# A new hand-out order for five engines: the same pieces, planned for four cases of TensorE's clock instead of three

## What is computed

```python
# L0 and L3: linear attention (16 or 8 heads)
q = softmax((xn @ Wq + bq).reshape(...), axis=-1)
k = softmax(masked(xn @ Wk + bk).reshape(...), axis=time)
y = einsum(q, einsum(k, v));  x = x + silu(film(layernorm(y))) @ W_out + b
# L1: softmax attention, 16 heads of 16, 256 x 256 scores
att = softmax(q @ k.T + mask, axis=2);  y = att @ v;  x = x + silu(film(layernorm(y))) @ out_w + b
# L2: two state space scans, forward and backward in time, E = 512 channels, N = 16 states
delta = softplus(dlt @ Wdt.T + bdt);  dA = exp(delta * A);  dBu = delta * B * u
h = dA * h + dBu;  y = sum_n(h * C)         # over 256 steps
out = (silu(mx) * (z1 + z2)) @ Wf.T + bf + skip;  x = x + gate * out
```

## Time and profile before

| | us |
|---|---|
| median of three runs | 4681.6 |
| the profiled execution | 4666.2 |
| its span, first to last instruction | 4664.4 |
| VectorE busy in it | 4085.4 |
| GpSimd busy | 3926.7 |
| TensorE busy | 3850.9 |
| ScalarE busy | 3671.9 |
| to the first scan | 436.7 |
| from there to the first scan of the last but one batch | 3937.0 |
| from there to the end | 290.7 |

### The profile page before, as it was taken

How to read it: one execution, slowest core, us unless ns; L and a number is a source line. 1 busy time by engine, 2 the same in 40 slices (tenths; PEclk the granted TensorE clock), 3 DMA queues, 4 the chain that set the end, 5 groups by cost and what they waited for, 6 DMA issues and landing times.

```text
span 4664.4 us, 73193 instructions
## 1 busy us (share of the span) xinstructions
PE 3850.9 (83%) x26068; PEld 2522.2 (54%) x26068; DVE 4085.4 (88%) x5552; ACT 3671.9 (79%) x8678; POOL 3926.7 (84%) x1836
## 2 busy tenths in 40 slices
PE   4867888888888889888888888888888888888665
PEld 3644555555555555555555555555555555555333
DVE  4313899999999999999999999999999999999985
ACT  0135788888898888888889888888888888888763
POOL 0003899999999999999999999999999999999995
PEclk7777899999999999999999999999999999999876
DMA  4002444444454444445454434445454444444441
GB/s 121 3 7 69 102 100 102 113 110 113 104 119 114 105 98 102 113 110 121 103 115 111 107 93 106 113 110 118 103 119 111 104 97 104 113 113 115 111 106 35
DMA packets 338585, 470.58 MB, mean 101 GB/s; under 512 B 56474, under 2 KB 166150, under 8 KB 338218
## 3 DMA queue, kind: packets, MB, share of 16 engines
q1 hardware_dynamic: 338218, 465.91, 42.9%
HBM read 378.71 MB, written 86.56 MB: 100 GB/s over the span
## 4 chain that ended last, share of the span: by engine, by line
PE 37%; ACT 25%; DVE 20%; POOL 8%; issue 7%; DMA 1%; SPq 0%; DVEq 0%; POOLq 0%; ACTq 0%
PE ps L170 14%; ACT ps L699 7%; DVE ps L714 6%; POOL S_X L758 5%; PE ps L375 5%; PE ps L394 4%; PE ps L793 4%; DVE S_X L714 4%; PE ps L160 3%; DVE A_sm L428 3%; POOL S_X L771 2%; DVE S_X L729 2%; PE ps L403 2%; PE ps L538 2%; ACT T_q L153 1%
## 5 line engine op out<-in xcount | busy, mean ns | idle before, releaser
L758 POOL TENSOR_TENSOR S_X<-S_slot,S_bc 128x1024 f32<-128x1024 f32 x1024 | 2392.0, 2361 | 33.3 <-PE ps L793 28.6
L699 ACT ACTIVATE ps<-S_slot,acol 128x256 f32<-128x256 f32 x4096 | 1736.2, 466 | 184.7 <-DVE S_X L729 127.2
L714 DVE TENSOR_TENSOR_SCAN ps<-ps,S_X 128x512 f32<-128x512 f32 x1088 | 1297.2, 1212 | 64.4 <-ACT ps L699 44.7
L714 DVE TENSOR_TENSOR_SCAN S_X<-ps,S_X 128x512 f32<-128x512 f32 x960 | 1148.7, 1208 | 31.3 <-ACT ps L699 24.8
L771 POOL TENSOR_TENSOR S_X<-S_X,S_bc 128x1024 f32<-128x1024 f32 x480 | 1132.7, 2363 | 49.7 <-DVE S_X L714 49.6
L729 DVE TENSOR_TENSOR S_X<-ps,S_bc 128x512 f32<-128x512 f32 x1088 | 724.0, 676 | 8.9
L793 PE MATMUL ps<-S_X,sum 128*32 128x256 f32 x8192 | 631.8, 412 | 38.8 <-POOL S_X L771 29.1
L394 PE MATMUL ps<-A_qP,A_kP 32*128 32x256 f32 x2048 | 338.2, 454 | 103.4 <-DMA A_qP<-A_ring 62.3
L428 DVE TENSOR_REDUCE A_sm<-ps 128x4 f32<-128x1024 f32 x256 | 312.7, 1222 | 95.9 <-PE ps L375 89.7
L793 PEld LDWEIGHTS ps<-S_X,sum 128*32 128x32 f32 x8192 | 203.0, 114 | 321.1 <-issue 186.4
L375 PE MATMUL ps<-A_kP,A_qP 32*128 32x256 f32 x2048 | 298.2, 409 | 52.4 <-DVE A_sm L428 32.4
(11 more groups left out here) (293 smaller groups left out, 7181.3 us busy)
## 6 DMA issues: line engine op xcount, KB each, us to landing
S_slot<-scr_dd SPq DMA_DIRECT2D x1024, 256.0 KB, 4.5
scr_dd<-C_dd SPq DMA_DIRECT2D x64, 1024.0 KB, 6.8
S_bc<-scr_bc SPq DMA_DIRECT2D x256, 256.0 KB, 6.6
L_xin<-in_x SPq DMA_DIRECT2D x32, 256.0 KB
C_mod<-scr_mod SPq DMA_DIRECT2D x32, 256.0 KB, 6.1
scr_x<-A_x SPq DMA_DIRECT2D x32, 256.0 KB, 5.8
T_x<-scr_x SPq DMA_DIRECT2D x32, 256.0 KB
out_x<-xs SPq DMA_DIRECT2D x32, 256.0 KB, 6.8
```

Source lines behind the costliest of these rows:

```text
L699: ins = a.activation(B["bank"][half_at(b, u, i)][:, n * T:(n + 1) * T], B["slot"][:, s, j, 0, :], ACT.Exp, scale=K.k["acol"][:, s, LINES * ...
L714: v.tensor_tensor_scan(line(x if u in ON_POOL else decay), line(decay), line(x), 0.0, ALU.mult, ALU.add).then_inc(S.scan.sem, 1)
L758: g.tensor_tensor(B["X"][:, u % RING], B["slot"][:, s, :, 1, :], rep(B["bc"][:, s, q, :], 1, LINES), ALU.mult).then_inc(S.b.sem, 1)
```

## The change

The diff touches only the strings. `FIRST` has new orders on every engine, from letter 110 on for TensorE, 142 for VectorE, 38 for ScalarE, 14 for GpSimd and 5 for the sync queue. The sync queue's `FIRST` is shorter by 11 letters, and its `TURN` begins at another place, so that the two join with no piece lost. Each `TURN` holds the same number of each letter as before. The number of instructions, their waits and their buffers are the same.

```diff
--- before.py
+++ after.py
@@ -1480,30 +1480,30 @@
 
 FIRST = {
     "PE": (
-        "WWWWWWWWWWWWWWWLLLLWLWWWWWLWWLWWWWWWWWWWWWWLWWWWWWLWWWWWWWWWWWWWLAAAAAAAAAAAAAAAAAAAAAAAAAALALLLALLLLLLAAAAAACACAACACACA"
-        "ACAAAAACAAAACAACAACCLALLCLALLLLLCLSASAAAAACACSASSACASCACAACASSASASASACASSASASASCASSACAACSSSSSCLASLSLCLSSALLSSLSSSSLLCSSS"
-        "LSTASAAAAACACSASSATCASC"),
+        "WWWWWWWWWWWWWWWLLLLWLWWWWWLWWLWWWWWWWWWWWWWLWWWWWWLWWWWWWWWWWWWWLAAAAAAAAAAAAAAAAAAAAAAAAAALALLLALLLLLLAAAAAAACACACACACA"
+        "ACAAAAACAAAACAACAACCLALLCLALLLLLCLSASAAAAASACSASCACSACACAACASSASASSASSACASASAACASSSACASASCSSCSSSLALSLSCLALSLSSLSSLSLCSSS"
+        "LSTASAAAAASACSASCACSATC"),
     "DVE": (
         "WWWWLWWWWWWWWWWWWWWWLWLWWWWLWLWWWWWWWWWWWWWWWWWLWWWWWWWWWWWWWWLWLWWWWWWWWWWWWWWWWWWWWWWWLWAWWWAAAAAAAAAAALLLLLLLLALACCAA"
-        "AAAAAACAAALLLLLLCLLASSPPLSASSPCSSPSCSPSSPASASASPAPSASASPASASSPGSCPSPSSSSPPSSSSPSPSSPSSPSSSPSPSSSPAGASPASLSPSSPSLLSSPLPSS"
-        "SLSGPPSSSSPSPLC"),
+        "AAAAAACAAALLLLLLCLLASPSLPASSSCPSPSSCSPSSPASASASPASPASASPASASSPGSCPSPSSSPSPSSSSPPSSSPSPSSSSPPSSGSSAPAPSASLSPSSPSLLSSPLSPS"
+        "SSLPSPGSSSPSLPC"),
     "ACT": (
-        "LLLWLLLLLLLLLLAAAAAAAAAAAAAAAAAAALLAALALALLLLLLLLLAACAAACAACCCCCCCACCAAAAACAACAAACCALLAACCLALALLLLCCCLLLLSLSCCCSCSSSASAC"
-        "SAASSACSAACSSCSSCSCSSCSCCSACCSSSASSASSASSASSACSASSSASCASSSASSSACSCSSASLSLSASSACSCLSALSASLSLSSLSLCSCSSSSC"),
-    "Pool": "LALCCCACSLSSSPCCCSSPSSSPSSSPSSPCSPSSSPPSSSSSSPPPSSSPSSAPSSPC",
-    "SP": "LAWWLAACCLACCCssCAsCsSCSLACSCCSStSssCAsCsSCSLACSCCSS",
+        "LLLWLLLLLLLLLLAAAAAAAAAAAAAAAAAAALLAAALALLLLLLLLLLAACAAACAACCCCCCCACCAAAACAAACAAACCALLACAALALLLLLCCCCLLLLLSSCSCSCCSASACA"
+        "SSSASASCAASCSSCCSSCCSSSSCCACSCSSASSASSASSASSCASASSSASCASSSASSSACSSCSSALSLSACSASALSASLSSSLLSSLSLSCCCCSSSS"),
+    "Pool": "LALCCCACSLSSSCPCCSSPSSPSSSSPSSPCSPSSSSPPSSSSSPPPSSSPSSAPSPSC",
+    "SP": "LAWWALACCCACLssCCACssCSSCASCLSStSssCCACss",
 }
 
 TURN = {
-    "PE": "ACATACASSATSASASTACASTSATSATSATSCATSSACAACSSSTSSCLASLSLCLSSALLSSLSSSSLLCSSSLSTASAAAAACACSASSATCASC",
+    "PE": "ACATACASSATSASSASSTACTASASTATATCASSSATCASASCSTSCSSSLALSLSCLALSLSSLSSLSLCSSSLSTASAAAAASACSASCACSATC",
     "DVE": (
-        "SLLSPSSPSPPASSGPPLSASSPCSTTSPSCTSPSSPASASASPAPSASASTPASTASSPTGSCPSPSTSSSPPSSSSPSPSTSPTTSSPSSSPSPSSSPAGASPASTLSPSSPSLLSSP"
-        "LPSSSLSGPPSSSSPSPLC"),
+        "LSLSAPSSPSPPSGPSLPASSSCPSTTTPSSCSPSSPASASASPASPASASTPATSASSPTGSCPSPSSSPSPTSSSSPPSSTSPTTSPSSSSPPSSGSSAPAPSASTLSPSSPSLLSSP"
+        "LSPSSSLPSPGSSSPSLPC"),
     "ACT": (
-        "LSLLLSLSCCCSCSSSASACSAASSACSAACSSTCSSTCSCSSCSCCTSACCSSSTASSASTSASSATSSACTSASSSASCTASSTSTASSSATCSTCSSASLSLSASSACSCLSALSAS"
-        "LSLSSLSLCSCSSSSC"),
-    "Pool": "SPSLSSSPCCCSSPSSSPSSSPSSPCSPSSSPPSSSSSSPTPPSSSPSSAPSSPC",
-    "SP": "tSssCTAsCsSCSLACSCCSS",
+        "LSLLLLSSCSCSCCSASACASSSASASCAASCSSCTCSSTCCSSSSCCTACSCSSASTSASSTASSASSTCATSASSSASCTASSSTASTSSATTCSSCSSALSLSACSASALSASLSSS"
+        "LLSSLSLSCCCCSSSS"),
+    "Pool": "SPSLSSSCPCCSSPSSPSSSSPSSPCSPSSSSPPSSSSSPTPPSSSPSSAPSPSC",
+    "SP": "CSSCASCLSStSssCTCACss",
 }
 
 ONCE = (w_pe, w_dve, w_act, w_sp)
```

## The result

The changed kernel takes 4566.1 us, the median of four runs (4562.65 to 4569.19), against 4681.0 us for the kernel before (4666.38 to 4683.03). The ratio is 0.9762, with a 95% interval of 0.9745 to 0.9778: 114.8 us, 2.4% less. The forecast was 4640 us with a range of 4598 to 4686.

The account below looks back on a forecast made before the run. VectorE was taken as leading, 95.1% busy in steady turns, waiting on chains through TensorE and ScalarE. Terms summed to 1.71 us per turn, taken as 1.2, times 28 turns 34 us: 4632, plus 8 offset, 4640; range 4598 to 4686.

Parts of the forecast that it names:

- A10's term: VectorE's reciprocal (L433) after the turned attention output: its wait goes, 0.80 us per turn, bounds 0 to 0.80.
- The maxima: VectorE's score maxima A2 to A7: the first one's wait goes, 0.26 us per turn, bounds 0 to 0.5.
- the sum cut from 1.71 to 1.2: All terms, us per turn: cut because VectorE, arriving earlier, would meet late exponentials at S41 to S43.
- T8 charged with +0.45: VectorE's masked state (L259): wait grows by about 0.45 us per turn, with S15 and S14 ahead on TensorE.
- S37: VectorE's scan, where ScalarE waits for TensorE's C8, moved ahead: its 0.76 us wait falls by 0.57 per turn.
- the clock term: Half-clock matmuls at TensorE's T5 in long turns: net 0 per long turn, bounds -1.0 to +2.2 us.
- GpSimd and the sync queue at 0: Moves in these two queues: counted 0, the sync queue with bounds -0.3 to 0.3 us per turn.
- T11's 0.39: VectorE's last add of a layer (L279): its wait goes, 0.39 us per turn, bounds 0 to 0.39.
- G4 and L9: For these, TensorE's S36 and L10 come about 0.35 us late, charged against the gain at scan S9.
- The waits only change places: Rival: new tight places on ScalarE return the gains; 0 to 0.3 us per turn, 4672 us, chance 0.23.
- The long turns go too: Rival: filled TensorE idle and S27 ahead of T5 keep the clock up or hide it; 4605 us, chance 0.16.
- The new turn falls into step with the clock: Rival: the half-clock stretch meets T5 in every turn, making the kernel slower; 4730 us, chance 0.11.

Follow-up runs that it names:

- the middle stretch: Kernel before with TensorE's stretch S10 to S16 and ScalarE's S27 to T7 in the changed kernel's order: 4633.9 us, ratio 0.9829, mean turn 129.80 us.
- Filling the wait: Kernel before with two float32 matmuls that nobody reads added ahead of A16's wait on TensorE: 4636.4 us, ratio 0.9921.
- The experiment: Changed kernel with GpSimd's and the sync queue's strings of the kernel before: 4590.9 us, ratio 0.9812.

## Why the prediction was wrong in size

**Right: the bound, and where the largest waits go.** VectorE's work of 124.7 us per turn stayed but for 0.4 us, and the waits in its turn were what there was to win. A10's term was 0.80, measured 0.79. In a plain turn of the changed kernel (timeline, columns as in rows 5):

```profile
1802.33 1.13 PE L394 MATMUL ps<-A_qP,A_kP 32*128 32x256 f32 x8 [1.78 <-ACT A_ring L471]
1803.39 1.11 PE L160 MATMUL ps<-ident,T_q 128*128 128x128 f32 x4
1804.29 3.16 PE L170 MATMUL ps<-C_xT,wcz 128*128 128x256 f32 x8
1807.38 1.93 PE L403 MATMUL ps<-A_ring,A_vA 128*32 128x256 f32 x32
1809.38 0.60 ACT L476 ACTIVATE A_kP<-ps 128x512 f32<-128x512 f32 x1
1811.44 0.35 DVE L433 RECIPROCAL A_srec<-ps 128x32 f32<-128x32 f32 x1
```

Beside the earlier trace rows: T10's row (L160) has no bracket where 2.02 us of waiting stood, the reciprocal has none where 1.17 stood. TensorE now waits 1.78 for exponential A16 in front of A24, because it arrives early. A24 takes 1.13 us in place of 2.08 and C9 3.16 in place of 3.78. In plain turns A24 starts 73.9 us after the turn's first scan, and 76.4 to 78.0 before, more than twice the 1.1 us that I had given it: the idle time in front of it is not the only one that was filled. The clock has a part in A10's gain as well: in most plain turns before, TensorE ran at the lower level from about 76 us on, behind T10's wait, and in the changed kernel this stretch is half as long. The maxima (0.26 predicted, 0.29 measured) and TensorE's wait before L9's product, which I said would stay, agree too; in the same turn of the changed kernel it is 5.0 us:

```profile
PE ps L160 <- ACT T_q L153: 5.0, 1, 5.0
```

**Wrong: the sum cut from 1.71 to 1.2.** I argued that VectorE, arriving earlier, meets exponentials with 0.35 to 0.5 us of margin. The waits of the terms I listed fell by 2.58 us per turn, more than the uncut sum. The margins were those of the old order. ScalarE's string had been moved with the others, and its own waits fell by 3.86 us per turn in total, which I didn't work out. The scans S41 to S43, which I had feared for, don't wait in the changed kernel. The cut cost 0.51 x 28 = 14 us of the error.

**Wrong: T8 charged with +0.45.** I counted the pieces that come in front of T8 on TensorE and not the waits that they fill. By the matched pieces TensorE waited 0.30 us before A17 and 0.60 before A19; both are 0 in the changed kernel. In plain turns T8 starts 64.4 us after the turn's first scan in place of 65.3 to 67.0, with more work in front. The wait on VectorE fell by 0.24, and T9's went (0.14). S37 gave 0.76, not 0.57. Together the two steps are mis-sized by 1.02 us per turn, the largest single part. Which piece brings T8 forward is open. The filled waits are not enough: with the middle stretch on two engines TensorE waits 0 before A17 and A19 as well, and T8's wait stays at 0.37; T6 alone took 0.08 off it. S12 and S13 ahead of T5 are needed, since T5 ahead of them brings the wait back from 0.13 to 0.43, but the middle stretch has them there too. S37's gain, in turn, needs only the middle stretch on two engines, which brought 0.62 of it.

**Wrong: the clock term at 0.** S27, S28 and S30 lost 0.59 us of waits per turn. The long turn of the changed kernel:

```profile
1647.75 1.13 PE L394 MATMUL ps<-A_qP,A_kP 32*128 32x256 f32 x8 [1.62 <-DMA A_qP<-A_ring]
...
1654.76 2.05 PE L170 MATMUL ps<-L3wv,T_xT 128*128 128x256 f32 x4
...
1657.93 0.84 ACT L302 ACTIVATE T_v<-ps,T_pc 128x256 f32<-128x256 f32 x2 [2.34 <-PE ps L170]
1660.83 1.22 DVE L714 TENSOR_TENSOR_SCAN S_X<-ps,S_X 128x512 f32<-128x512 f32 x1 [1.87 <-ACT ps L699]
```

The wait for the DMA and T5 at 2.05 us stay, as predicted. T5 on ScalarE still delays a scan, now S28 with 1.87 in place of S27 with 1.38, but S30 hardly waits, and the price of a long turn fell from 2.9 to 2.3 us. They are 6 of 24. A middle kind of 128.4 us (3 of 24) has its price at T4, in the timeline of the middle turn:

```profile
1380.03 1.97 PE L170 MATMUL ps<-L3wq,T_xT 128*128 128x256 f32 x4
...
1383.97 0.69 DVE L245 TENSOR_REDUCE T_qm<-ps 128x16 f32<-128x512 f32 x1 [1.46 <-PE ps L170]
```

My bounds were -1.0 to +2.2 per long turn, but I took the middle of them, and I took the clock's price in the kernel before from the length of its longer turns alone, 24.7 us. Filling the wait gave 37 us on median times in the same kernel. Plain turns hold groups at 2.08 us too, and by comparing them with long ones I couldn't see that; with the wait filled, turns as short as 128.1 us appear in the kernel before.

**Wrong: GpSimd and the sync queue at 0.** I looked at each moved piece's margin in the old order. In the new one their strings are worth 25 to 31 us. In the table they have no row of their own: the wait that they prevent at L7 is in neither kernel. The experiment shows it only because it combines new and old.

**Wrong: two smaller terms.** T11's 0.39 didn't come. G4 and L9, charged with 0.35 for A13's new place, don't wait in the changed kernel (0.02 and 0.00), while VectorE's string without the others made them wait 0.49 and 0.40, so the charge was true for the old TensorE and false for the new. The 0.45 us of VectorE's busy time I didn't expect at all: I had written that its 124.7 us stay, because the instructions are the same, but an instruction's duration and its overlap with the next one are not fixed by the program.

**The error in one line.** Per turn 0.51 cut, 1.02 at T8 and S37, 0.59 clock and 0.45 busy time, less 0.13 for the rest, is 2.44 us, times 28 turns 68. The first four turns, not among the 24, gave back 3 of it, lead-in and end another 2. The offset between profile and median, of which I kept 8 us, turned to -3: 11 more. That is 74 us, or 4640 less 4566.

**The rivals.** "The waits only change places" fits the edits on one engine of the kernel before (T10 or T6 on TensorE, VectorE's or ScalarE's order, and S27 by its turns, though not by its ratio) and is false of all together. "The long turns go too" was nearest in size, at 4605. But the long turns stayed, and what it missed was the waits of the plain turn. "The new turn falls into step with the clock" happened in neither profiled execution; with T6 ahead of A19 (16 of 24 turns long) something of the kind did, and cost 0.3%. The slowest runs of the kernel before may be of this kind: 4724 us is 58 above its profiled execution, as much as 20 more turns that are 2.9 us longer (an estimate; none of these runs has a profile).

**Still open.** Where T8's gain comes from, as said above, and why the product at L824 takes less time, isn't tested. The 7.5 us of the lead-in are no effect of the change: to the first scan, the eight profiled kernels with the old `FIRST` on all engines took 435.0 to 444.6 us, mean 440.1, and the seven with the new one 436.6 to 444.2, mean 440.0.

## What to carry to other kernels

Price a new order against itself and not against the old one, since margins and waits of the old order don't hold in the new. One way, which no run here tests: for every engine, walk the new string with the measured durations and let each piece start at the later of its releases and its neighbour. If orders of several engines were planned together, one engine's part alone tells little: here the whole strings of VectorE or ScalarE alone lost 0.6 and 1.0%. Judge the plan only as a whole. A wait of a microsecond or two on TensorE in front of a chain is worth a try at filling it with matmuls that nobody reads, once the rows behind it show durations that double; it gave 0.8 and 0.3% here.

## What the hardware showed that I had not expected

The kernel before has no single time. Over all its runs here it took 4665 us at a mean granted clock of 0.903 and 4724 at 0.889, and between these the time goes up as the clock goes down, with some scatter (4680 at 0.900, 4699 at 0.897). That is 1.3% with not one instruction changed. The chip alone isn't the reason: on one and the same chip its median was 4675.3 in one session and 4698.8 in a later one. The changed kernel took 4560 to 4569 at 0.906 to 0.910 in its eight runs. So, as far as eight runs in two sessions tell, the change also removed most of the spread, and that is why its ratio is 0.9762 in one session and 0.9716 in another. The Trainium skill, in "TensorE: Matmul & The Clock Gate", Part 1 on the HAM clock gate, says that one and the same kernel shows a different number of slow matmuls from run to run, depending on the phase at its start. The runs here agree, with granted clocks of 0.889 to 0.907 for one kernel. Its figure of under 1% of a span is for the ramp at a kernel's start, and not for what is seen here, stretches at the lower level in every turn.

A group's duration at the two levels is 1.13 and 2.08 us here, while the granted clock averages 0.95 over the turn. The mean hides it: 12.4 us of a turn of 127.6 are at the lower level, and that is enough to stretch one chain by a microsecond.
